# GpSimd makes the layer-norm scalings and the third bf16 parts of queries, keys and maxima, instead of VectorE

## The chip, the cores and the metric

One core of one Trainium2 chip runs the whole program. The metric is the device time of one execution in microseconds (us); the time of a kernel is the median of its runs.

## The reference

The reference is one transformer layer over 16 sequences of 512 tokens of 128 channels, in float32.

```
x = x + attention(layernorm(x))      # 16 heads of 8 channels, band |i - j| <= 128
x = x + ffn(layernorm(x))            # product-key experts: 8 heads, 32 x 32 keys, top 8 of 1024

attention:  softmax(q k^T / sqrt(8), masked to the band) v, then a 128x128 projection
layernorm:  (x - mean) / sqrt(var + 1e-5) over the 128 channels, no gain and no offset
ffn:        batch norm over all tokens, scores of 1024 experts in 8 heads, the best 8 of each,
            softmax weights times gelu of the expert products, summed
```

## The kernel before

The program has two stages that follow each other: `attention` (some 795 us of the profiled span), then `ffn`. The change touches `attention` alone.

`attention` is a software pipeline over sequences. Each engine has its own program, written out by hand; they meet through semaphores. Each engine runs steps t = -1 to 17 (t = 2 to 13 in a loop), and within a step 16 slots h = 0 to 15, one for each head. In step t three sequences are in work:

- sequence t: its scores (`scores`, L474 and L478) go to PSUM tiles SX and SY, and VectorE takes the row maxima of each head from them (two reductions, L395 and L397, in each slot). Each of the two PSUM tiles is single, so TensorE may write head h+1 into it only when VectorE has reduced head h.
- sequence t-1: its transposed scores (`scoresT`, L505) go to TX and TY, ScalarE takes the exponentials into PT (L340, L342), GpSimd sets what lies outside the band to zero (`mask`, L250, four instructions a head), and TensorE multiplies by the values (`values`, L531) for groups of four heads in slots 6, 10, 14 and 2 of the next step.
- sequence t+1 is prepared: layer-norm statistics (`stats`, slots 0 and 1), the variance to the power -1/2 on GpSimd (L258, slot 1), the scaling to xn (`norm`, L374, four instructions of 128x128, slot 3), the transposes of xn (slot 4), then the products q (slot 5) and k (slot 6). Sequence t-2 is finished: its attention output is divided by the softmax sums (L433, L435, slots 3, 7, 8 and 10), turned, projected, added to the input (L443), normalised again (`stats` in slot 13, L272 on GpSimd, `norm` in slot 14) and turned once more (slot 15).

Queries, keys and row maxima are used as sums of three bf16 parts, so that a bf16 product has the precision wanted. Part 1 is a rounding by ScalarE (L299, L351); VectorE subtracts it, which gives the rest (L421, L380); ScalarE rounds the rest to part 2 (L302, L353); VectorE subtracts once more and writes part 3 (L426 for q and k in slots 6 and 7, L383 for the maxima in slots 1 and 9). SyncE then stores the parts to memory and loads them back, rearranged, into Q and K (`back`, 24 transfers a step) and into three rows of Q (`shift_rows`). Each store waits for the third part.

All small products of a step (turned maxima, att0 to att3, xnT, q, k, at, pj, v, x2T) share one PSUM bank, MB. Each may write it only when the one before it in a fixed order has been read; that order is the list SHARED, and `bank_free` makes the wait. Here att0 (slot 3), read by L435, is ahead of xnT (slot 4); att1 (slot 7), read by L435, is ahead of att2 (slot 8).

Every engine works strictly in the order of its own program, so that a wait holds back all that is queued behind it.

Of the kernel before, what the change touches and what calls it, by code (L numbers as in the profile page):

```python
# [30 lines left out]
ALU = mybir.AluOpType  # L31
# [3 lines left out]
SEQS = 16  # L35
# [15 lines left out]
def attention(nc, ctx, x, w_qkvT, w_projT, identb, band, w_q, keysT, idf, bnst, KM, extra, x1_out, x2T_out):  # L51
# [186 lines left out]
    @block.gpsimd  # L238
    def _(pool):
        nc.gpsimd.memset(half[:, :], -0.5).then_inc(S["v_pads_set"], 1)  # L240
        for b in range(2):
            nc.gpsimd.memset(V[b][:, :, :, :], 0.0).then_inc(S["v_pads_set"], 1)
        pool.wait_ge(S["v_pads_set"], 3)
        for b in range(2):
            nc.gpsimd.memset(V[b][:, :, :, DK:DK + 1], 1.0).then_inc(S["v_pads_set"], 1)

        def mask(out, pairs, stop_low):

            s = 1 if stop_low else -1
            return nc.gpsimd.affine_select(out=out, in_=out, compare_op=ALU.is_ge, fill=0.0, base=0,  # L250
                                           pattern=([[0, 2]] if pairs else []) + [[s, P]], channel_multiplier=-s)

        def step(t, c):
            for h in range(H):

                if h == 1 and 0 <= c + 1 < SEQS:
                    pool.wait_ge(S["x_variance"], t + 2)
                    nc.gpsimd.tensor_tensor(rs[:, :], ve[:, :], half[:, :], ALU.pow).then_inc(S["x_rstd"], 1)  # L258

                if 0 <= c - 1 < SEQS:  # L260
                    pt = PT[:, h % 8, :]
                    y = pt[:, 512:1280].rearrange("p (j n) -> p j n", j=2)
                    await_(pool, S["outer_exp"], (t - 1) * H + h + 1)
                    mask(pt[:, 128:256], False, False).then_inc(S["exp_masked"], 1)
                    mask(pt[:, 256:384], False, True).then_inc(S["exp_masked"], 1)
                    await_(pool, S["inner_exp"], (t - 1) * H + h + 1)
                    mask(y[:, :, 0:128], True, True).then_inc(S["exp_masked"], 1)
                    mask(y[:, :, 256:384], True, False).then_inc(S["exp_masked"], 1)

                if h == 13 and 0 <= c - 2 < SEQS:  # L270
                    pool.wait_ge(S["x1_variance"], t - 1)
                    nc.gpsimd.tensor_tensor(trs[:, :], te[:, :], half[:, :], ALU.pow).then_inc(S["x1_rstd"], 1)  # L272

        steps(pool, step)

# [82 lines left out]
    def _(dve):  # L358
# [10 lines left out]
            dve.wait_ge(s2, (s + 1) * TILES)  # L369
            nc.vector.tensor_scalar(ae[:, :], av[:, :, 1], EPS, None, ALU.add).then_inc(to, 1)  # L370

        def norm(src, av, r, dst, to):
            for i in range(TILES):
                o = nc.vector.tensor_scalar(dst[:, i, :], src[:, i, :], av[:, i, 0:1], r[:, i:i + 1], ALU.subtract, ALU.mult)  # L374
            o.then_inc(to, 1)

        def shift(s, nth):

            dve.wait_ge(S["max_part1"], s * 2 + nth)
            nc.vector.scalar_tensor_tensor(out=rm[:, :].rearrange("p (i n) -> p i n", n=P), in0=MB[0:8, :, :], scalar=-1.0,  # L380
                                           in1=mp[:, 0, :].rearrange("p (i n) -> p i n", n=P), op0=ALU.mult, op1=ALU.subtract).then_inc(S["max_rest"], 1)
            dve.wait_ge(S["max_part2"], s * 2 + nth)
            nc.vector.tensor_tensor(mp[:, 2, :], rm[:, :], mp[:, 1, :], ALU.subtract).then_inc(S["max_part3"], 1)  # L383

        def step(t, c):
            b = c % 2
            for h in range(H):
                if 0 <= c < SEQS:
                    n = t * H + h + 1
                    dve.wait_ge(S["outer_scores"], n)  # L390
                    if h == 0 and c >= 1:
                        dve.wait_ge(S["maxima_turned"], t * 2 - 1)
                    if h == 8 and c >= 1:
                        dve.wait_ge(S["maxima_turned"], t * 2)
                    nc.vector.tensor_reduce(mx[:, h, 0:4:3], SX[:, :, :], AX.X, ALU.max).then_inc(S["outer_maxima"], 1)  # L395
                    dve.wait_ge(S["inner_scores"], n)
                    nc.vector.tensor_reduce(mx[:, h, 1:3], SY[:, :, 0:384], AX.X, ALU.max).then_inc(S["inner_maxima"], 1)  # L397

                if h == 1 and 0 <= c - 1 < SEQS:
                    shift(t - 1, 2)  # L400
                if h == 9 and 0 <= c < SEQS:
                    shift(t, 1)

                if h == 0 and 0 <= c + 1 < SEQS:
                    dve.wait_ge(S["x_loaded"], 16 * (t + 2))
                    stats(0, t + 1, xin[1 - b], st6, mv, ve, S["x_stats"], S["x_means"], S["x_variance"])
                if h == 1 and 0 <= c + 1 < SEQS:
                    stats(1, t + 1, xin[1 - b], st6, mv, ve, S["x_stats"], S["x_means"], S["x_variance"])
                if h == 3 and 0 <= c + 1 < SEQS:
                    dve.wait_ge(S["x_rstd"], t + 2)  # L410
                    if c >= 0:
                        dve.wait_ge(S["xn_turned"], t + 1)
                    norm(xin[1 - b], mv, rs, xn, S["xn_ready"])
                if c == -1 and h in (4, 7):

                    both = K[0 if h == 4 else 1][64:P, :, :].rearrange("p h n -> p (h n)").bitcast(F32)
                    nc.vector.memset(both, TWO_ONES).then_inc(S["k_ones_set"], 1)
                for hh, nm, dst, r, sc in ((5, "q", qp, rq, DK ** -0.5), (6, "k", kp, rk, 1.0)):
                    if h == hh and 0 <= c + 1 < SEQS:
                        dve.wait_ge(S[nm + "_part1"], t + 2)  # L420
                        nc.vector.scalar_tensor_tensor(out=r[:, :].rearrange("p (i n) -> p i n", n=P), in0=MB[:, :, :], scalar=sc,  # L421
                                                       in1=dst[:, 0, :].rearrange("p (i n) -> p i n", n=P),
                                                       op0=ALU.mult, op1=ALU.subtract).then_inc(S[nm + "_rest"], 1)
                    if h == hh + 1 and 0 <= c + 1 < SEQS:
                        dve.wait_ge(S[nm + "_part2"], t + 2)
                        nc.vector.tensor_tensor(dst[:, 2, :], r[:, :], dst[:, 1, :], ALU.subtract).then_inc(S[nm + "_part3"], 1)  # L426

                for i, sl in enumerate(ASLOT):
                    if h == sl and 0 <= c - 2 < SEQS:
                        n = (t - 2) * 4 + i + 1  # L430
                        dve.wait_ge(S["att_turned"], n)
                        hv = MB[:, :, :].rearrange("p g (h e) -> p (g h) e", e=SLOT_V)
                        nc.vector.reciprocal(rec[:, i, :], hv[:, :, DK]).then_inc(S["sums_inverted"], 1)  # L433
                        dve.wait_ge(S["sums_inverted"], n)
                        nc.vector.tensor_tensor(A[:, i, :].rearrange("p (h d) -> p h d", d=DK), hv[:, :, 0:DK],  # L435
                                                rec[:, i, :].unsqueeze(2).broadcast_to([P, H, DK]), ALU.mult).then_inc(S["att_normed"], 1)

                if h == 12 and 0 <= c - 2 < SEQS:
                    dve.wait_ge(S["projected"], t - 1)
                    dve.wait_ge(S["residual_loaded"], 16 * (t - 1))  # L440
                    if c - 2 >= 1:
                        dve.wait_ge(S["x1_stored"], 16 * (t - 2))
                    nc.vector.tensor_tensor(X1[:, :, :], MB[:, :, :], xres[:, :, :], ALU.add).then_inc(S["x1_ready"], 1)  # L443
                if h == 13 and 0 <= c - 2 < SEQS:
                    dve.wait_ge(S["x1_ready"], t - 1)
                    stats(0, t - 2, X1, t6, tv, te, S["x1_stats"], S["x1_means"], S["x1_variance"])
                    stats(1, t - 2, X1, t6, tv, te, S["x1_stats"], S["x1_means"], S["x1_variance"])
                if h == 14 and 0 <= c - 2 < SEQS:
                    dve.wait_ge(S["x1_rstd"], t - 1)
                    norm(X1, tv, trs, X2, S["x2_ready"])  # L450

            if 0 <= c - 2 < SEQS:
                dve.wait_ge(S["x2T_ready"], t - 1)
                nc.vector.bn_stats(bnst[:, t - 2, :] if isinstance(t, int) else bnst[:, bass.ds(t - 2, 1), :].rearrange("p o n -> p (o n)"), X2T[:, :]).then_inc(S["bn_stats_ready"], 1)
# [603 lines left out]
```

## Time and profile before

| | |
|---|---|
| median of 3 runs | 1863.76 us (1862.04 to 1866.11) |
| the profiled execution, its own time | 1866.48 us |
| its span | 1864.7 us |
| TensorE (PE) busy | 1573.5 us, 84% |
| VectorE (DVE) busy | 1521.5 us, 82% |
| ScalarE (ACT) busy | 1303.6 us, 70% |
| GpSimd (POOL) busy | 1329.2 us, 71% |

The shares are means over both stages. The page's slices show that from the third to the fifteenth slice of 40 (the full steps of `attention`) PE is busy for nine tenths or more, DVE for eight tenths, ACT for six and POOL for five; in `ffn` POOL is the fullest with nine tenths. A matmul's end is modelled in the profile and reaches past the start of the next one, so short stops of PE are read from the distance between starts, set against the same distance where nothing was awaited.

### The profile page before, as it was taken

Reading aid. Unit: us, or ns where it says so; the run is one execution under the profiler, and the core shown is the slowest. Engines: PE = TensorE matmul, PEld = TensorE weight load, DVE = VectorE, ACT = ScalarE, POOL = GpSimd, SP = SyncE. Lnnn points to the kernel's source line nnn. Section 1 sums busy time; section 2 is a strip of 40 time slices with the busy share of each in tenths; the row PEclk is TensorE's granted clock in tenths of the full one; section 3 lists DMA queues with packets and bytes.
Section 4 is the critical chain, followed back from the end, with each engine's and each line's share of the span. In section 5 each row is a group of like instructions: output and inputs, shape, how many; then the busy total and the mean of one; then the engine's idle time right before and its main releaser. Section 6 shows DMA issues by size and latency. Waiting matters only on the chain.

```text
span 1864.7 us, 38400 instructions
## 1 busy us (share of the span) xinstructions
PE 1573.5 (84%) x11936; PEld 1135.9 (61%) x11936; DVE 1521.5 (82%) x3784; ACT 1303.6 (70%) x1773; POOL 1329.2 (71%) x1579
## 2 busy tenths in 40 slices
PE   3899999999999999677887878788788787887877
PEld 2456566666666665346666666666666566666666
DVE  3778888888888886268898889888788898888888
ACT  1266666666666666368788787788778788787885
POOL 1055555555555555379999989989898898898995
PEclk9699999999999999789899999899899998998999
DMA  5334344444444442010000000000000000000000
GB/s 137 78 82 94 93 101 98 96 106 98 99 96 97 94 99 47 24 34 1 18 18 18 2 17 17 2 17 17 7 12 17 18 1 17 18 0 17 12 7 6
DMA packets 70876, 85.39 MB, mean 46 GB/s; under 512 B 6528, under 2 KB 61056, under 8 KB 66048
## 3 DMA queue, kind: packets, MB, share of 16 engines
q1 hardware_dynamic: 70752, 84.08, 19.2%
q8 instruction: 36, 0.59, 0.1%
q14 instruction: 88, 0.72, 0.1%
HBM read 58.10 MB, written 25.95 MB: 45 GB/s over the span
## 4 chain that ended last, share of the span: by engine, by line
DVE 18%; issue 17%; ACT 12%; PE 6%; POOL 3%; DVEq 1%; ACTq 0%; DMA 0%; POOLq 0%
DVE W L930 12%; ACT E L838 8%; PE WT L997 4%; POOL SUM L738 3%; ACT L773 2%; PE MB L940 2%; DVE M8Y L874 1%; DVE SMALL L891 1%; DVE SMALL L874 1%; DVE CT L913 1%; PE MB L943 1%; ACT L772 1%; ACT LZ L806 0%; PE E L953 0%; DVEq L698 0%
## 5 line engine op out<-in xcount | busy, mean ns | idle before, releaser
L738 POOL TENSOR_TENSOR SUM<-SIM 128x1024 f32<-128x1024 f32 x512 | 959.2, 1915 | 87.4 <-ACT SIM L766 77.7
L930 DVE SCALAR_TENSOR_TENSOR W<-SUM,SMALL,E 128x1024 f32<-128x1024 f32 x512 | 646.6, 1279 | 60.4 <-ACT E L838 51.7
L838 ACT ACTIVATE E<-SUM,NB 128x1024 f32<-128x1024 f32 x512 | 567.2, 1117 | 160.8 <-DVE W L930 120.2
L997 PEld LDWEIGHTS WT<-idf,W 128*128 128x128 f32 x4096 | 494.7, 150 | 232.6 <-issue 153.7
L997 PE MATMUL WT<-idf,W 128*128 128x128 f32 x4096 | 557.7, 289 | 78.7 <-DVE CT L913 57.0
L250 POOL TENSOR_SCALAR_AFFINE_SELECT PT<-PT 128x128 f32<-128x128 f32 (+1 forms) x1024 | 334.0, 352 | 314.0 <-ACT PT L340 280.0
L397 DVE TENSOR_REDUCE mx<-SY 128x2 f32<-128x768 f32 x256 | 242.5, 947 | 8.6 <-PE SY L478 8.4
L395 DVE TENSOR_REDUCE mx<-SX 128x2 f32<-128x512 f32 x256 | 175.2, 684 | 75.1 <-PE SX L478 74.4
L342 ACT ACTIVATE PT<-TY 128x768 f32<-128x768 f32 x256 | 207.6, 811 | 2.4 <-PE TY L505 0.7
L940 PE MATMUL MB<-KM,BNT 128*128 128x512 f32 x128 | 84.7, 748 | 121.1 <-ACT OUT L786 121.1
L340 ACT ACTIVATE PT<-TX 128x512 f32<-128x512 f32 x256 | 153.5, 600 | 45.0 <-PE TX L505 44.4
L474 PE MATMUL SY<-K,Q 72*128 72x384 bf16 x512 | 163.5, 342 | 10.8 <-DVE mx L397 10.5
L531 PE MATMUL PV<-PT,V 128*32 128x384 f32 (+1 forms) x2048 | 154.9, 444 | 2.3 <-POOL PT L250 2.3
L478 PE MATMUL SY<-bandb,idb 128*128 128x128 bf16 x1024 | 146.4, 225 | 0.0
L505 PE MATMUL TY<-Q,K 75*128 75x384 bf16 x512 | 127.1, 330 | 6.0 <-ACT PT L342 5.5
L943 PE MATMUL MB<-X2T,KI 128*128 128x512 f32 x240 | 128.0, 616 | 2.1 <-ACT SIM L766 1.9
L478 PEld LDWEIGHTS SY<-bandb,idb 128*128 128x128 bf16 x1024 | 103.8, 101 | 39.9 <-issue 6.1
L964 PE MATMUL MB<-KO,CT 128*128 128x128 f32 x1024 | 126.9, 278 | 1.1 <-DVE CT L913 1.1
L964 PEld LDWEIGHTS MB<-KO,CT 128*128 128x128 f32 x1024 | 121.7, 195 | 1.3 <-DVE CT L913 1.3
L474 PE MATMUL SX<-K,Q 72*128 72x256 bf16 x512 | 102.6, 282 | 18.3 <-DMA Q<-q_parts 14.9
L531 PEld LDWEIGHTS PV<-PT,V 128*32 128x32 f32 x2048 | 60.8, 111 | 83.1 <-issue 55.2
L319 ACT COPY U<-PV 128x512 f32<-128x512 f32 x64 | 37.4, 585 | 96.4 <-PE PV L531 96.4
(106 smaller groups left out, 1817.1 us busy)
## 6 DMA issues: line engine op xcount, KB each, us to landing
K<-k_parts SPq DMA_DIRECT2D x96, 192.0 KB
Q<-q_parts SPq DMA_DIRECT2D x288, 64.0 KB
q_parts<-qp SPq DMA_DIRECT2D x16, 384.0 KB, 2.4
k_parts<-kp SPq DMA_DIRECT2D x16, 384.0 KB, 2.4
xin<-in_x SPq DMA_DIRECT2D x16, 256.0 KB, 3.1
xres<-in_x SPq DMA_DIRECT2D x16, 256.0 KB, 9.3
x<-X SPq DMA_DIRECT2D x16, 256.0 KB, 2.2
x2T<-X2T SPq DMA_DIRECT2D x16, 256.0 KB, 2.1
```

The lines of the kernel that those rows point to most:

```text
L250: return nc.gpsimd.affine_select(out=out, in_=out, compare_op=ALU.is_ge, fill=0.0, base=0, pattern=([[0, 2]] if pairs else []) + [[s, P]], ...
L342: nc.scalar.activation(pt[:, 512:1280].rearrange("p (j n) -> p j n", j=2), TY[:, :, 0:384], ACT.Exp).then_inc(S["inner_exp"], 1)
L395: nc.vector.tensor_reduce(mx[:, h, 0:4:3], SX[:, :, :], AX.X, ALU.max).then_inc(S["outer_maxima"], 1)
L397: nc.vector.tensor_reduce(mx[:, h, 1:3], SY[:, :, 0:384], AX.X, ALU.max).then_inc(S["inner_maxima"], 1)
L474: pe.matmul(out, Q[b][0:KQ, h, i * P:(i + 1) * P], K[b][0:KQ, h, k0 * P:k1 * P], start=clear, stop=False, skip_group_check=True)
L478: return pe.matmul(out, idb[:, :], band_, start=False, stop=True, skip_group_check=True)
L531: o = pe.matmul(PV[32 * e:32 * e + 32, q0 * P:q1 * P], V[b][:, j, h, :], PT[:, h % 8, at:at + (q1 - q0) * P], start=(j == 0), stop=(j == 3 ...
L738: return eng.tensor_tensor(SUM[(q * FH + h) % RING][:, :].rearrange("p (i j) -> p i j", i=NK), sx, sy, ALU.add)
L838: nc.scalar.activation(E[h % 2][:, :], SUM[(k * FH + h) % RING][:, :], ACT.Exp, bias=NB[q][:, h:h + 1]).then_inc(S["exp_ready"], 1)
L930: nc.vector.scalar_tensor_tensor(out=W[h % WRING][:, :], in0=SUM[(k * FH + h) % RING][:, :], scalar=TOP[q][:, h, TOPK - 1:TOPK], in1=E[h % ...
L964: o = pe.matmul(po, CT[k % 2][:, e, :], key_out[:, e, :], start=False, stop=(e == BLK - 1))
L997: o = pe.matmul(WT[:, e, :], W[h % WRING][:, e * P:(e + 1) * P], ident[:, :], is_transpose=True, start=(h == 0 and e % 4 == 0), stop=(h == ...
```

## The change

The third parts (two for the maxima and one each for q and k in a step) and both layer-norm scalings (four instructions of 128x128 each) move from VectorE to GpSimd. No arithmetic changes. On GpSimd the scaling to xn stands in slot 2, the third part of the upper maxima behind it, both ahead of the masks of that slot; the third parts of q, k and the lower maxima stand ahead of the masks of slots 6, 7 and 10; the second power and the scaling to X2 stand ahead of the masks of slot 14 (the power stood behind those of slot 13, which is the same place). VectorE gets waits so that it does not overwrite what GpSimd still reads.

```diff
@@ gpsimd
+        def norm(src, av, r, dst, to):
+            for i in range(TILES):
+                o = nc.gpsimd.tensor_scalar(dst[:, i, :], src[:, i, :], av[:, i, 0:1], r[:, i:i + 1], ALU.subtract, ALU.mult)
+            o.then_inc(to, 1)
+
+        def shift(s, nth):
+
+            pool.wait_ge(S["max_part2"], s * 2 + nth)
+            nc.gpsimd.tensor_tensor(mp[:, 2, :], rm[:, :], mp[:, 1, :], ALU.subtract).then_inc(S["max_part3"], 1)
...
+                if h == 2 and 0 <= c + 1 < SEQS:
+                    if c >= 0:
+                        await_(pool, S["xn_turned"], t + 1)
+                    await_(pool, S["x_rstd"], t + 2)
+                    norm(xin[1 - (c % 2)], mv, rs, xn, S["xn_ready"])
+
+                if h == 2 and 0 <= c - 1 < SEQS:
+                    shift(t - 1, 2)
+                if h == 10 and 0 <= c < SEQS:
+                    shift(t, 1)
+                for hh, nm, dst, r in ((6, "q", qp, rq), (7, "k", kp, rk)):
+                    if h == hh and 0 <= c + 1 < SEQS:
+                        pool.wait_ge(S[nm + "_part2"], t + 2)
+                        nc.gpsimd.tensor_tensor(dst[:, 2, :], r[:, :], dst[:, 1, :], ALU.subtract).then_inc(S[nm + "_part3"], 1)
+
+                if h == 14 and 0 <= c - 2 < SEQS:
+                    pool.wait_ge(S["x1_variance"], t - 1)
+                    nc.gpsimd.tensor_tensor(trs[:, :], te[:, :], half[:, :], ALU.pow).then_inc(S["x1_rstd"], 1)
+                    if c - 2 >= 1:
+                        await_(pool, S["x2_turned"], t - 2)
+                    await_(pool, S["x1_rstd"], t - 1)
+                    norm(X1, tv, trs, X2, S["x2_ready"])
...
-                if h == 13 and 0 <= c - 2 < SEQS:
-                    pool.wait_ge(S["x1_variance"], t - 1)
-                    nc.gpsimd.tensor_tensor(trs[:, :], te[:, :], half[:, :], ALU.pow).then_inc(S["x1_rstd"], 1)
@@ vector
         def shift(s, nth):
 
             dve.wait_ge(S["max_part1"], s * 2 + nth)
+            prev = s * 2 + nth - 1
+            if not isinstance(prev, int) or prev >= 1:
+                dve.wait_ge(S["max_part3"], prev)
...
-            dve.wait_ge(S["max_part2"], s * 2 + nth)
-            nc.vector.tensor_tensor(mp[:, 2, :], rm[:, :], mp[:, 1, :], ALU.subtract).then_inc(S["max_part3"], 1)
...
                 if h == 1 and 0 <= c + 1 < SEQS:
+                    if c >= 0:
+                        dve.wait_ge(S["xn_ready"], t + 1)
                     stats(1, t + 1, xin[1 - b], st6, mv, ve, S["x_stats"], S["x_means"], S["x_variance"])
-                if h == 3 and 0 <= c + 1 < SEQS:
-                    dve.wait_ge(S["x_rstd"], t + 2)
-                    if c >= 0:
-                        dve.wait_ge(S["xn_turned"], t + 1)
-                    norm(xin[1 - b], mv, rs, xn, S["xn_ready"])
...
+                        if c >= 0:
+                            dve.wait_ge(S[nm + "_part3"], t + 1)
...
-                    if h == hh + 1 and 0 <= c + 1 < SEQS:
-                        dve.wait_ge(S[nm + "_part2"], t + 2)
-                        nc.vector.tensor_tensor(dst[:, 2, :], r[:, :], dst[:, 1, :], ALU.subtract).then_inc(S[nm + "_part3"], 1)
...
+                        dve.wait_ge(S["x2_ready"], t - 2)
...
-                if h == 14 and 0 <= c - 2 < SEQS:
-                    dve.wait_ge(S["x1_rstd"], t - 1)
-                    norm(X1, tv, trs, X2, S["x2_ready"])
```

## Rows read from the trace of the kernel before

**Rows 1.** Stretches by window: length, then busy us of each engine (instructions), PEclk.
```profile
391.29:435.23 43.94, 41.86 (x392) 27.04 (x392) 37.35 (x77) 28.86 (x49) 22.84 (x67) 1.00 0.43 98
```
**Rows 2.** Line L454, once a step: duration ns min/median/max, first and last start.
```profile
L454 DVEq FUSED_REGOPS  x12: 64/64/64, 169.5 to 652.7; - x12
```
**Rows 3.** Timeline of PE in that step: start us, us, engine, line, out<-in.
```profile
399.99 0.28 PE L478 MATMUL SY<-bandb,idb 128*128 128x128 bf16 x2
401.12 0.65 PE L558 MATMUL MB<-idf,xn 128*128 128x128 f32 x4 [0.85 <-DVE A L435]
...
402.96 0.28 PE L478 MATMUL SY<-bandb,idb 128*128 128x128 bf16 x2
403.07 1.08 PE L563 MATMUL MB<-xnT,wq 128*128 128x512 f32 x2
...
406.70 2.36 PE L531 MATMUL PV<-PT,V 128*32 128x256 f32 x32
...
412.20 0.28 PE L478 MATMUL SY<-bandb,idb 128*128 128x128 bf16 x2
412.93 0.66 PE L588 MATMUL MB<-idf,U 128*128 128x128 f32 x4 [0.45 <-DVE A L435]
...
431.82 0.61 PE L605 MATMUL MB<-idf,X 128*128 128x128 f32 x4
...
432.81 0.38 PE L474 MATMUL SX<-K,Q 72*128 72x256 bf16 x2
```
**Rows 4.** Timeline of DVE around the two stops of PE, and slot 14.
```profile
399.30 1.20 DVE L374 TENSOR_SCALAR xn<-xin,mv,rs 128x128 f32<-128x128 f32 x4
...
400.42 0.25 DVE L433 RECIPROCAL rec<-MB 128x16 f32<-128x16 f32 x1
400.69 0.29 DVE L435 TENSOR_TENSOR A<-MB,rec 128x128 f32<-128x128 f32 x1
...
411.55 0.83 DVE L426 TENSOR_TENSOR kp<-rk,kp 128x512 bf16<-128x512 f32 x1
...
412.58 0.29 DVE L435 TENSOR_TENSOR A<-MB,rec 128x128 f32<-128x128 f32 x1
...
430.49 1.12 DVE L374 TENSOR_SCALAR X<-X,tv,trs 128x128 f32<-128x128 f32 x4 [0.67 <-POOL trs L272]
```
**Rows 5.** Timeline in slots 1 and 2 (DVE, POOL) and slot 14 (POOL).
```profile
394.94 0.68 DVE L383 TENSOR_TENSOR mp<-rm,mp 8x512 bf16<-8x512 f32 x1 [0.69 <-ACT mp L353]
...
396.19 1.01 POOL L258 TENSOR_TENSOR rs<-ve,half 128x4 f32<-128x4 f32 x1 [3.55 <-DVE ve L370]
...
429.45 1.01 POOL L272 TENSOR_TENSOR trs<-te,half 128x4 f32<-128x4 f32 x1
```
**Rows 6.** Groups by line and form, whole span: busy us, mean ns.
```profile
L738 POOL TENSOR_TENSOR SUM<-SIM 128x1024 f32<-128x1024 f32 x512 | 959.2, 1915 | 87.4 <-ACT SIM L766 77.7 <-DVE W L930 9.6
...
L250 POOL TENSOR_SCALAR_AFFINE_SELECT PT<-PT 128x256 f32<-128x256 f32 x512 | 195.8, 406 | 33.6 <-ACT PT L342 28.0
L250 POOL TENSOR_SCALAR_AFFINE_SELECT PT<-PT 128x128 f32<-128x128 f32 x512 | 141.4, 297 | 280.3 <-ACT PT L340 280.0 <-issue 0.3
...
L426 DVE TENSOR_TENSOR kp<-rk,kp 128x512 bf16<-128x512 f32 x16 | 13.0, 815 | 0.0
...
L426 DVE TENSOR_TENSOR qp<-rq,qp 128x512 bf16<-128x512 f32 x16 | 10.9, 681 | 0.7 <-ACT qp L302 0.7
```
**Rows 7.** Timeline of the start: ACT, DVE, SyncE's queue (SPq) and PE.
```profile
17.80 0.62 ACT L302 CAST kp<-rk 128x512 bf16<-128x512 f32 x1 [0.76 <-DVE rk L421]
...
18.68 3.47 DVE L417 MEMSET K<- 64x4096 f32 x1 [0.91 <-issue]
22.18 0.69 DVE L426 TENSOR_TENSOR kp<-rk,kp 128x512 bf16<-128x512 f32 x1
...
39.80 0.59 PE L474 MATMUL SX<-K,Q 72*128 72x256 bf16 x2 [14.87 <-DMA Q<-q_parts]
```

More of the change, by code:

```diff
@@ L370, in stats @@
             nc.vector.tensor_scalar(ae[:, :], av[:, :, 1], EPS, None, ALU.add).then_inc(to, 1)
[L372 to L375, printed above, removed]
         def shift(s, nth):
             dve.wait_ge(S["max_part1"], s * 2 + nth)
+            prev = s * 2 + nth - 1
+            if not isinstance(prev, int) or prev >= 1:
+                dve.wait_ge(S["max_part3"], prev)
             nc.vector.scalar_tensor_tensor(out=rm[:, :].rearrange("p (i n) -> p i n", n=P), in0=MB[0:8, :, :], scalar=-1.0,
                                            in1=mp[:, 0, :].rearrange("p (i n) -> p i n", n=P), op0=ALU.mult, op1=ALU.subtract).then_inc(S["max_rest"], 1)
-            dve.wait_ge(S["max_part2"], s * 2 + nth)
-            nc.vector.tensor_tensor(mp[:, 2, :], rm[:, :], mp[:, 1, :], ALU.subtract).then_inc(S["max_part3"], 1)
         def step(t, c):
```

## The prediction

> **What bounds the kernel now.** I read the page's slices first: they split the run into `attention` and `ffn`, and the change leaves `ffn` as it is, so all that counts is the length of the attention steps. Next I took one full step by window [rows 1]: 43.94 us, with PE busy 41.86, DVE 37.35, ACT 28.86 and POOL 22.84. The start of the once-a-step line L454 says that this step is typical: 12 starts from 169.5 to 652.7 us are 11 distances of 43.93 us [rows 2]. PE is nearly full at a granted clock of 1.00, so a gain can only be what PE loses in stops. Then I went down PE's timeline of the step and compared distances between starts. Where nothing is awaited, the line of the last two mask products of a head (L478) is followed 0.11 us later by the next one (402.96 to 403.07 [rows 3]). From 399.99 to the transposes of xn it takes 1.13, so 1.02 us are lost; from 412.20 to the transposes of att2 it takes 0.73, so 0.62 are lost [rows 3]. Both lines name the division L435 on DVE as the releaser. Seven smaller excesses of the same kind, which I read off in the same way, are 0.05 to 0.4 us each; all together some 3.6 us a step, of which I count below only what the change reaches. That is the reading: PE sets the pace, and DVE stops it in two places.
>
> **What is taken from DVE.** Each step loses two scalings (1.20 and 1.12 us), the third parts of q and k (0.68 and 0.83) and two of the maxima (0.68 each) [rows 4 to 6], some 5 us, and with them the stops of DVE ahead of the maxima's part (0.69 [rows 5], twice) and ahead of the scaling in slot 14 (0.67 [rows 4]). Most of it buys nothing, as DVE waits for PE elsewhere. Where it counts:
> - Slots 3 and 4. The scaling to xn runs from 399.30 and pushes the reciprocal to 400.42 and L435 to 400.69 + 0.29 = 400.98; PE starts at 401.12, 0.14 later [rows 3, 4]. Without the scaling the pair of 0.56 us starts at about 399.3 and PE is released at 400.0, ahead of the 400.10 at which it would come. All 1.02 us go, if xn itself is there.
> - Slots 7 and 8. Without kp (from 411.55) L435 ends at 412.1 and not at 412.87 [rows 4], ahead of PE's 412.31. The 0.62 go.
> - Small stops behind L383 (0.09 in slot 3) and around slots 9 and 10 (0.06 to 0.14, four of them) go too, 0.45 together. But with DVE relieved, the next thing late is the chain ACT part 1, DVE rest, att3 around slots 9 and 10; I give 0.35 back for it, and 0.1 for others. Sum of this edit: 1.02 + 0.62 + 0.45 - 0.45 = 1.64 us a step.
>
> **What is put on POOL, and what waits for it.** No row shows a scaling on POOL. Nearest are its masks, one input and no scalar from memory: 297 ns for 128x128 and 406 for 128x256 [rows 6], and in a row of eight they follow each other faster than that. The other end is the power of 128x4, 1.01 us although it has four elements a row [rows 5], a fixed cost that a costly function can have. So a scaling is 0.26 to 1.0 us; I take c = 0.35, near the mask, whose shape it has, with something for two scalars. A subtraction of 512 elements is between the mask's rate (about 0.6 us) and the 1915 ns of a 128x1024 sum scaled by size with its fixed cost, 1.1 us [rows 6]; I take 1.05.
> - xn, slot 2. With L383 gone from DVE (394.94 to 395.6), the variance and thus the power come 1.3 us earlier, 394.9 in place of 396.19 [rows 5]. Then POOL masks head 1 until about 397.05, scales until 397.05 + 4c = 398.45, and PE can take it 0.15 later, against its 400.10. Free as long as c is below 0.72. Behind it wait the third part of the maxima (to 399.6) and the masks of heads 2 and 3, done by 402.3, where the value product takes them at 406.70 [rows 3]: 4 us of cover, so they cost nothing. If that cover were gone, each us late would be a us of PE.
> - X2, slot 14. This has no cover. The power ends at 429.45 + 1.01 = 430.46 [rows 5]; DVE then scaled until 431.61, PE turned X2 at 431.82 without waiting [rows 3, 4]. POOL is done at 430.5 + 4c, and PE released 0.15 later (by c = 0.35: 432.05). The stop is 4c - 1.17 us, here 0.23. The copy to X2T, and DVE's statistics on it ahead of its next reduction, move by the same amount, so it isn't counted twice.
> - Third parts of q and k. POOL comes to k's part behind the masks of head 6, some 0.6 us later than DVE did, q's 0.4. SyncE's stores, and the loads `back` behind them, go as much later. In the timeline of SyncE those loads are issued by 420 and the transfers thin out by 428.5, while PE's next step starts at 432.81 [rows 3]: 4 us of cover. The part of the lower maxima gets 2 us later; its store stands in the queue behind those same loads anyway. The part of the upper ones gets 4 us later, with a cover of 10 us until slot 8. All nothing.
> - The new waits on DVE (the previous third part, the previous scaling) are for things done a third of a step earlier, and cost nothing; behind them would stand the reductions.
>
> The SBUF page of the Trainium skill (SBUF — State Buffer, Who interferes with whom) says that a VectorE instruction with two SBUF inputs and a GpSimd instruction that reads SBUF block each other for the whole instruction. The trace agrees in kind: kp, which overlaps a mask, takes 815 ns, qp 681 [rows 6]. The change takes the last such instructions off DVE in these steps, so by the rule no new contention arises; it changes nothing in the sum.
>
> **The steps summed.** A full step: 1.64 - 0.23 = 1.4 us. Thirteen steps (t = 2 to 14) have both stops: 18.2 us. Steps 0 and 1 have the scaling without the division ahead of it: 1.5 together. In the start, kp's third part stands on DVE behind a memset from 18.68 (3.47 us) and runs at 22.18, though ACT had part 2 at 18.42 [rows 7]; the store of it, then the loads, then PE's first scores at 39.80 hang on it [rows 7]. On POOL, 0.3 us later for the scaling and 1.05 long, it is done at 19.9 and not 22.87: 2.5 us won, taking the loads to move with it. The last three steps lose the stop in slot 14 and its like in serial work: 1.0. Sum: 18.2 + 1.5 + 2.5 - 1.0 = 21.2 us. The profiled execution took 1866.48 us and would take 1845.3; it is 2.7 us above the median of the runs, 1863.76, and from that I get 1842.5 us, 1.1% less.
>
> **The rivals.**
> - GpSimd becomes the bound in slot 14, slower than before. The price is c: the stop 4c - 1.17 eats the 1.64 at c = 0.70, from there the kernel is slower. With c = 1.0, the row of the power, the stop in slot 14 is 2.8, and xn comes at 401.2, a stop of 1.1 where 1.02 was, so that of the 1.64 only 0.6 stays: 2.8 + 0.1 - 0.6 = 2.3 us a step, 30 in all, and some 8 in the last three steps: 1900. For it speaks only the power's row; against it the masks, which are whole instructions on 128x128 at 0.3. The GPSIMD Engine Reference of the Trainium skill (Engine selection) says to leave elementwise work to VectorE, GpSimd being about twice as slow with two inputs and near line rate with one; our two-input subtraction is covered, so by that page too slot 14 decides. Chance 0.13.
> - A middle c of 0.5 to 0.65: a stop of 0.8 to 1.4, 0.2 to 0.8 us won a step: 3 to 11 us and 1 to 2 from the start: 1852 to 1860. Chance 0.15.
> - The transfers become the bound: the cover of 4 us ahead of slot 0 is thinner than it looks, and PE waits for heads 0 to 7 what it had won. The window's DMA share of 0.43 [rows 1] is against it. Within 3 us of 1864. Chance 0.07.
> - The change doesn't do what it says, as GpSimd needs other code for scalings than for masks and loads it each time: two loads a step, no row has their price. In the trace POOL alternates between masks and powers with nothing between them, so I give it 0.03; slower by an unknown amount, over 20 us.
> - PE wins more: the stops of slots 1 and 2 behind DVE's reductions (0.41 and 0.34, from the timeline) go too. Up to 0.75 us in 13 steps: 1833. Chance 0.12.
> - The forecast, 1837 to 1850: 0.50.
>
> **Numbers.** A difference of 0.2% (3.7 us) is about what a measurement of this kernel can tell from none. Faster by more than that: 0.50 + 0.12 + nearly all of the middle case, 0.13: 0.75. Within it: 0.02 + 0.06: 0.08. Slower: 0.13 + 0.03 + 0.01: 0.17. The range has to leave out the slow rivals (0.16) and takes in the other cases: 1830 to 1862.
>
> **What would show it.** In the profile after: PE's transposes of xn and of att2 follow L478 after 0.11 us, with no stop named A; the step by L454 is 42.5 us; DVE busy in a step falls to about 32.5 and POOL rises to about 30; kp's third part is stored at about 20 us and the first scores start at 37. A scaling on POOL above 0.70 us, or a stop of PE ahead of the turned X2 of over 1.6 us, would show the forecast wrong; so would value products that wait for masks, or scores that wait for DMA.

## The result and the profile after

The changed kernel takes 1884.24 us in the median of its four runs, where the kernel before took 1862.9. One of the four, of 1918.5 us, ran in a slower state with a lower granted clock (0.913 against 0.937 to 0.942) and is left out of the ratio, so that 1881.47 us stands against 1862.9: 1.0096, with a 95% interval of 1.0069 to 1.0124. The change is slower by about 1%; the forecast was 1842.5, and the range ended at 1862. The profiled execution took 1881.47 us, its span is 1879.8.

The stages moved in opposite ways. The attention stage ends where the first instruction of `ffn` on VectorE starts: 795.5 us before, 816.5 after, 21.0 us later. `ffn`, whose code is the same, took 1069.2 us before and 1063.3 after. That second number moves by itself from kernel to kernel (more below), so what follows is about the 21 us.

The once-a-step line, which answers to [rows 2] (it is L472 now); columns: duration ns min/median/max, first and last start us:

```profile
L472 DVEq FUSED_REGOPS  x12: 64/64/64, 164.2 to 660.7; - x12
```

Eleven steps take 496.5 us, 45.14 each, where they took 43.93. The first start is 5.3 us earlier than before, so the start of the kernel gained the 4 us of the forecast and more, and the steps lost it. The groups by line and form, whole span (busy us, mean ns, idle before and its releaser), for what GpSimd got; they answer to [rows 6]:

```profile
L250 POOL TENSOR_SCALAR_AFFINE_SELECT PT<-PT 128x128 f32<-128x128 f32 x512 | 139.2, 293 | 154.7 <-ACT PT L368 154.5
...
L255 POOL TENSOR_SCALAR xn<-xin,mv,rs 128x128 f32<-128x128 f32 x64 | 50.3, 801 | 0.4 <-POOL rs L268 0.4
L255 POOL TENSOR_SCALAR X<-X,tv,trs 128x128 f32<-128x128 f32 x64 | 50.2, 798 | 3.4 <-POOL trs L286 3.4
...
L261 POOL TENSOR_TENSOR mp<-rm,mp 8x512 bf16<-8x512 f32 x32 | 36.8, 1149 | 5.6 <-ACT mp L381 5.6
...
L282 POOL TENSOR_TENSOR kp<-rk,kp 128x512 bf16<-128x512 f32 x16 | 18.6, 1162 | 3.7 <-ACT kp L330 3.7
...
L623 PE MATMUL MB<-idf,X 128*128 128x128 f32 x64 | 11.5, 310 | 38.1 <-POOL X L255 38.1
```

A scaling of 128x128 takes 0.8 us on GpSimd, nearly three masks of the same shape. The last row is the price: PE stood still for 38.1 us ahead of the transposes of X2 and waited for that scaling. One such place, in the timeline of PE and POOL (start us, us, engine, line, out<-in, idle before and its releaser), answers to slot 15 in [rows 3] and to slot 14 in [rows 4, 5]:

```profile
388.03 1.03 POOL L286 TENSOR_TENSOR trs<-te,half 128x4 f32<-128x4 f32 x1
389.27 3.14 POOL L255 TENSOR_SCALAR X<-X,tv,trs 128x128 f32<-128x128 f32 x4 [0.21 <-POOL trs L286]
...
390.29 0.28 PE L496 MATMUL SY<-bandb,idb 128*128 128x128 bf16 x2
...
392.56 0.63 PE L623 MATMUL MB<-idf,X 128*128 128x128 f32 x4 [1.99 <-POOL X L255]
```

Slots 3 and 4, and att2, in the same views, answer to the two stops in [rows 3]:

```profile
401.76 3.14 POOL L255 TENSOR_SCALAR xn<-xin,mv,rs 128x128 f32<-128x128 f32 x4
...
404.55 0.28 PE L496 MATMUL SY<-bandb,idb 128*128 128x128 bf16 x2
404.96 0.66 PE L576 MATMUL MB<-idf,xn 128*128 128x128 f32 x4
...
416.01 0.28 PE L496 MATMUL SY<-bandb,idb 128*128 128x128 bf16 x2
416.13 0.60 PE L606 MATMUL MB<-idf,U 128*128 128x128 f32 x4
```

The distance ahead of att2 is 0.12 us, the free one; ahead of xn it is 0.41 where it was 1.13. Both stops that VectorE made are gone as forecast; at xn a stop of 0.3 us is left, which GpSimd makes. From one turned X2 to the next (392.56 to 437.04) it is 44.48 us; but the mean step is 45.14. The difference is in the granted clock. Rows by window: length, busy us (instructions) of PE, PEld, DVE, ACT and POOL, then PEclk (1.00, 0.50, 1.00), DMA share, GB/s:

```profile
200.00:209.00 9.00, 7.47 (x78) 4.88 (x75) 6.48 (x16) 4.88 (x8) 6.65 (x14) 1.00 0.32 80
211.00:220.00 9.00, 9.00 (x53) 5.32 (x54) 7.22 (x17) 4.66 (x8) 4.81 (x13) 0.50 0.71 143
222.00:231.00 9.00, 8.94 (x72) 5.94 (x72) 7.02 (x11) 7.26 (x13) 7.30 (x19) 1.00 0.15 27
```

From 210.7 to 221 us TensorE ran at 0.50, 1.2 GHz in place of 2.4. The stop before it ended at 209.46. The step from there to the next turned X2 (257.33) took 47.87 us, 3.4 more than the 44.48 of a step without a fall; the steps with the falls at 163.0 and 258.5 us took 46.77 and 46.26, 2.3 and 1.8 more. In the kernel before there is no such fall from 100 to 740 us; in the changed one there are four, at 163.0, 210.7, 258.5 and 705.7, each 0.3 to 2 us behind a stop of 1.99 us (162.69, 209.46, 257.33, 703.84), and one more behind that of 749.95. The nine stops between were followed by none. These counts, like those of every kernel below, are from one profiled execution.

### The profile page after: what moved, and what is told of

Same layout as the page of the kernel before. It is cut to its first block, busy times and chain, and to the rows that moved or that the text cites. A ratio compares the mean times of both kernels' runs of the same rounds, so it can differ in the third digit from the quotient of the medians.

```text
span 1879.8 us, 38549 instructions
## 1 busy us (share of the span) xinstructions
PE 1575.7 (84%) x11936; PEld 1139.1 (61%) x11936; DVE 1447.0 (77%) x3592; ACT 1304.9 (69%) x1773; POOL 1494.7 (80%) x1771
## 4 chain that ended last, share of the span: by engine, by line
issue 14%; DVE 14%; POOL 12%; ACT 9%; PE 6%; DVEq 0%; ACTq 0%; POOLq 0%; DMA 0%
POOL SUM L756 12%; DVE W L948 9%; ACT E L856 6%; PE WT L1015 3%; PE MB L958 2%; ACT L791 2%; DVE M8Y L892 1%; DVE SMALL L909 1%; PE MB L961 1%; DVE SMALL L892 1%; DVE CT L931 1%; PE E L971 0%; ACT LZ L824 0%; ACT SIM L784 0%; ACT L790 0%
## 5 line engine op out<-in xcount | busy, mean ns | idle before, releaser
L1015 PEld LDWEIGHTS WT<-idf,W 128*128 128x128 f32 x4096 | 486.5, 148 | 226.5 <-issue 149.4
L1015 PE MATMUL WT<-idf,W 128*128 128x128 f32 x4096 | 550.4, 286 | 72.2 <-DVE CT L931 52.8
L250 POOL TENSOR_SCALAR_AFFINE_SELECT PT<-PT 128x128 f32<-128x128 f32 (+1 forms) x1024 | 328.1, 350 | 178.2 <-ACT PT L368 154.5
L523 PE MATMUL TY<-Q,K 75*128 75x384 bf16 x512 | 131.0, 339 | 5.6 <-ACT PT L370 5.3
```

What stands on the lines that cost most here:

```text
L1015: o = pe.matmul(WT[:, e, :], W[h % WRING][:, e * P:(e + 1) * P], ident[:, :], is_transpose=True, start=(h == 0 and e % 4 == 0), stop=(h == ...
```

## The experiments

Theory A: the whole loss is the scaling to X2. Nothing covers it in slot 14, it stops TensorE for 2 us, and a stop like that can be followed by a fall of the clock. Rival B: it is GpSimd's load as a whole, with the later third parts and stores. Rival C: the clock falls for a reason of its own.

**e1 and e9: X2 back on VectorE.**

```diff
@@ gpsimd, slot 14
...
-                    await_(pool, S["x1_rstd"], t - 1)
-                    norm(X1, tv, trs, X2, S["x2_ready"])
@@ vector
...
+                if h == 14 and 0 <= c - 2 < SEQS:
+                    dve.wait_ge(S["x1_rstd"], t - 1)
+                    norm(X1, tv, trs, X2, S["x2_ready"])
```

> The changed kernel, but the scaling to X2 is made by VectorE in slot 14 again; the scaling to xn and the third parts stay on GpSimd. Theory A (the whole loss is the scaling to X2: a scaling on GpSimd takes 0.78 us and not 0.35, nothing covers it in slot 14, TensorE stops 1.99 us there, and after such a stop its clock sometimes falls to half): no stop over 0.3 us ahead of the turned X2, no stretch at half clock in the full steps, a step of about 42.5 us in place of 44.5, and the prediction's sum without its slot-14 term: about 1840 us. Rival B (it is GpSimd's load as a whole, or the later third parts and their stores): most of the loss stays, 1865 to 1880 us.

Measured: 1854.96 us, ratio 0.9926 (0.9901 to 0.9952). The step is (628.4 - 163.4) / 11 = 42.27 us, from the once-a-step line:

```profile
L475 DVEq FUSED_REGOPS  x12: 64/64/64, 163.4 to 628.4; - x12
```

There is no stop of 1 us or more in the full steps and no fall between 100 and 720 us; att2 and X2 are released without a stop, and xn costs PEld 0.3:

```profile
DVE X L398 <- POOL trs L286: 5.5, 8, 0.7
...
PEld MB L579 <- POOL xn L255: 2.1, 8, 0.3
```

These are waits from 280 to 620 us (total, times, longest); the first is VectorE's 0.7 us for the power, as before. All of the mechanism came as theory A says, and B falls: one scaling moved back turns a loss of 1% into a gain. But the total is 15 us above the expected 1840 (10 by the ratio, as the kernel before took 1867.59 us beside it): the attention stage ended 24.3 us earlier (771.2), and `ffn` took 1078.4 us in place of 1069.2. In this run and the next ones a ratio is to the kernel before as it ran beside them.

**e2: X2 alone on GpSimd**, the rest as in the kernel before.

> The kernel before with the scaling to X2 alone moved to GpSimd. Theory A: the two stops that VectorE made (1.02 and 0.62 us) stay, and 1.95 us are added: a step of 45.9 us, 25 us in 13 steps, some 6 in the last ones, and 3.3 for each fall of the clock (2 to 5 of them): 1898 to 1912 us. Rival B: with GpSimd's load but a third of that added by the change and the stores where they were, close to 1863 us, at most 1870.

Measured: 1944.92 us, ratio 1.0432 (1.039 to 1.0473). The direction is A's, the size is not. A step without a fall is 46.13 us (219.02 to 265.15), 2.2 above before, as expected. But ten of the twelve stops from 169 to 711 us have a fall in their last 0.3 us or up to 1.2 us behind, not 2 to 5 in all, and each costs 1.9 to 5.2 us (360.89 to 408.93 is 48.04; 169.37 to 219.02 is 49.65; 505.18 to 556.49 is 51.31). The mean step is 49.2. So falls are most of this kernel's loss, and how many there are does not follow from the length of the stop, which is the same 1.95 us here as in the changed kernel with 4 of 13. In the rows one sees a stop, and the matmuls behind it at 1.5 to 1.7 times their length, with twice the distance from start to start (0.42 from TX to TY, where a step without a fall has 0.22):

```profile
556.49 1.09 PE L618 MATMUL MB<-idf,X 128*128 128x128 f32 x4 [1.95 <-POOL X L255]
557.37 0.64 PE L518 MATMUL TX<-Q,K 75*128 75x256 bf16 x2
557.79 0.85 PE L518 MATMUL TY<-Q,K 75*128 75x384 bf16 x2
...
265.62 0.38 PE L518 MATMUL TX<-Q,K 75*128 75x256 bf16 x2
265.84 0.49 PE L518 MATMUL TY<-Q,K 75*128 75x384 bf16 x2
```

**e3: only the third parts on GpSimd.**

> The changed kernel with both scalings back on VectorE; only the third parts are made by GpSimd. Theory A: the stop of 0.62 us ahead of att2 goes and the 1.02 ahead of xn stays, a step of about 43.3 us, 8 us in 13 steps, and some 3 at the start, as k's third part no longer stands behind the memset: about 1852 us. Rival B (later third parts hold back the stores and loads): 1863 us or more, with TensorE waiting for DMA ahead of slot 0 or 8.

Measured: 1857.45 us, ratio 0.9948 (0.9926 to 0.997); the step is 43.05 us, 0.25 shorter than expected. Its profiled execution took 1843.41 us, the fastest of the six, so that the profile shows more gain than the median. In the full steps TensorE doesn't wait for DMA ahead of any slot. The later third parts cost nothing.

**e4 and e6: the stop filled with work.** e4 has 16 transposes of the identity ahead of the wait for X2, e6 four products of 128x512 (this is e6's edit):

```diff
                     bank_free(pe, "x2T", t, c)
+                    for i in range(4):
+                        pe.matmul(MB[:, :, :], idf[:, :], KT[:, :], start=True, stop=True)
                     pe.wait_ge(S["x2_ready"], t - 1)
```

> The changed kernel, with 16 transposes of the identity (some 1.8 us of TensorE work whose result is overwritten) in slot 15 between the wait for the bank and the wait for X2, so that TensorE works through the stop. Theory A with the stop as the cause of the clock's fall: no stretch at half clock in the full steps, the step stays at about 44.5 us, and the 3.3 us of each fall are won: 1866 to 1874 us. Rival C (the clock falls there for another reason): falls as before, 1880 to 1887 us.

> The changed kernel with its stop filled again, but by four products of 128x512 in place of 16 transposes, so that TensorE's program grows by 8 instructions a slot 15 and not by 32. In e4 the program's growth brought a stop of 2.6 us without a releaser at the loop's end, with a fall behind it, where the filled stops had none. Theory A: no such stop here, no falls in the full steps, a step of 44.5 us, and of the changed kernel's loss the part of the falls (4 or 5 of 3.4 us) is won: 1.000 to 1.004 of the kernel before. If the falls come whatever fills the stop: 1.01.

Measured: e4 1894.59 us, ratio 1.0137 (1.0111 to 1.0162); e6 1898.93 us, ratio 1.0189 (1.0143 to 1.0236). Neither won anything, and both lie above what either theory expected. In e6 the filling was mis-sized: a product of 128x512 in f32 is two passes (the "x2" of L563 in [rows 3] is one product), so it ran for 3.65 us and not for 1.84. And both bring a new stop that names no releaser, in each second step, behind slot 15 of the loop's last step. In e4:

```profile
208.36 1.92 PE L622 MATMUL MB<-idf 128*128 128x128 f32 x16
210.40 0.66 PE L625 MATMUL MB<-idf,X 128*128 128x128 f32 x4
210.90 0.38 PE L523 MATMUL TX<-Q,K 75*128 75x256 bf16 x2
211.12 0.49 PE L523 MATMUL TY<-Q,K 75*128 75x384 bf16 x2
214.28 0.61 PE L492 MATMUL SX<-K,Q 72*128 72x256 bf16 x2 [2.68 <-issue]
```

As a clean test of the filling they fail, yet they tell about the clock. In e4 there are five falls between 200 and 600 us, and five stops of the new kind (2.5 to 2.7 us): each fall is with one of them, and the filled places, in the steps between too, have none. GpSimd has no part in these stops. In e6 the new stops are 1.1 to 1.7 us, five of them, with three falls, behind the longer three (1.39, 1.39, 1.68).

**e5, e7, e8: the length of the scaling to X2 as a dial.** e5 shares it, two tiles on each engine at once. e7 makes it in two instructions of 128x512 with broadcast operands. e8 scales by constants (subtract 0, multiply by 1), so that it leaves the normalising of X2 out and its result is not the layer's. This is e7's edit:

```diff
-                    norm(X1, tv, trs, X2, S["x2_ready"])
+                    nc.gpsimd.tensor_tensor(X2[:, :, :], X1[:, :, :], tv[:, :, 0:1].broadcast_to([P, TILES, P]), ALU.subtract).then_inc(S["x2_centred"], 1)
+                    await_(pool, S["x2_centred"], t - 1)
+                    nc.gpsimd.tensor_tensor(X2[:, :, :], X2[:, :, :], trs[:, :].unsqueeze(2).broadcast_to([P, TILES, P]), ALU.mult).then_inc(S["x2_ready"], 1)
```

> The changed kernel, with the scaling to X2 shared: two tiles on GpSimd and two on VectorE, at the same time. Theory A (the stop is 4c - 1.17 us with c = 0.78, and falls of the clock follow stops of about 2 us): with 2c in place of 4c and the 0.17 that GpSimd waits for its own power, the stop is 0.5 to 0.6 us, the step 42.27 (e1) + 0.55 = 42.8 us, no falls in the full steps: some 8 us above e1, 0.995 to 0.999 of the kernel before. Were the loss from moving any of the scaling off VectorE, and not from its length, it would be near the changed kernel, 1.01.

> The changed kernel, with the scaling to X2 on GpSimd as two instructions of 128x512 (subtract the mean, then multiply, each with a broadcast operand) in place of four of 128x128. From the 1.15 us that a third part takes, and 0.2 for the wait between the two: 2.5 us in place of 3.14, a stop of about 1.35 us in place of 1.99, a step of 43.9 us. If a broadcast operand costs more, up to 3.5 us and a longer stop.

> The changed kernel, with the scaling to X2 by constants (subtract 0, multiply by 1) and not by two scalars from memory, so X2 is the unscaled sum. It asks what the 0.8 us of a scaling are. If reading the two scalars makes them, an instruction falls to the 0.3 us of a 128x128 mask, the scaling to X2 ends before TensorE wants it, no stop in slot 15, a step near 42.3 us. If it is the operation itself, 0.7 to 0.8 us and the stop of 1.99 stay. The four on xn keep their scalars, for comparison.

The three kernels, with the changed one and e1 around them; the stop is the idle time of PE ahead of X2's transposes:

| kernel | scaling to X2 on GpSimd | stop | step | falls, 150 to 710 us | ratio to before |
|---|---|---|---|---|---|
| after | 4 x 0.78 = 3.14 us | 1.99 | 44.48 without a fall, 45.14 mean | 4 | 1.0096 |
| e8 | 4 x 0.62 = 2.48 us | 1.31 | 43.80 | 0 | 1.001, a single run |
| e7 | 1.04 + 0.2 + 1.04 = 2.28 us | 1.06 | 43.53 | 0 | 1.0006, a single run |
| e5 | 1.71 us | 0.55 | 43.12 | 0 | 0.9957 (0.9936 to 0.9978) |
| e1 | none | 0 | 42.27 | 0 | 0.9926 (0.9901 to 0.9952) |

The dial is straight over the first four rows: the step less the stop is 42.49, 42.49, 42.47 and 42.57 us. e1, with no stop, lies 0.2 to 0.3 us below that line, which is not explained. A scaling of 0.78 us gives 44.48, above the 43.93 of before; one of 0.62 gives 43.80, below it. e7's halves are cheaper than expected (1.04, not 1.15) and its single run of 1862.25 us is the time of the kernel before, 1861.19 beside it; e8's is 1863.06. For e8 the answer to its question is: mostly the operation itself. Without scalars from memory an instruction is 643 ns and not 798; the mask's 0.3 us isn't reached:

```profile
L255 POOL TENSOR_SCALAR xn<-xin,mv,rs 128x128 f32<-128x128 f32 x64 | 50.1, 794 | 0.4 <-POOL rs L268 0.4
L291 POOL TENSOR_SCALAR X<-X 128x128 f32<-128x128 f32 x64 | 39.7, 643 | 3.2 <-POOL trs L286 3.2
```

**e10: the scaling to xn in two instructions**, X2 on VectorE; and e9, the kernel of e1 again beside it.

> The kernel of e1 once more, on another chip and in 5 rounds. In e1's profile the attention stage ended 24.4 us earlier than before, but the whole was only 15 us shorter, since the ffn stage, the same code, took 1078 us and not 1069. If that length is drawn anew in each execution (over the profiles so far it goes from 1062 to 1078 with its mean granted clock, 0.94 to 0.924), this profile shows the same attention stage, 771 us, and another ffn, 1062 to 1072, and the ratio comes out at about 0.988. If an earlier and fuller attention stage makes ffn slower, ffn is again near 1078 and the ratio 0.9926.

> e1 with the scaling to xn, on GpSimd, as two instructions of 128x512 with a broadcast operand, as e7 had for X2 (2.3 us in place of 3.13). TensorE's last stop there, 0.3 us ahead of the transposes of xn, goes; a step of 42.0 to 42.1 us in place of 42.27 and 0.8 us at the start: 3 to 4 us less than e9.

Measured: e9 1852.19 us, ratio 0.9922 (0.9894 to 0.995); e10 1846.27 us, ratio 0.9899 (0.9873 to 0.9926). e10's step is (620.8 - 158.8) / 11 = 42.0 us, as expected; PE waits no more for xn, and it is 6 us faster than e9 where 3 to 4 were expected. (In the two profiled executions the difference is 2 us: the attention stage is 8 shorter and `ffn` 6 longer.) In e9 the attention stage ended at 769.8 and `ffn` took 1075.5 us; in e10 761.6 and 1081.7. The long `ffn` of e1 is no accident of one execution: e9 is the same kernel.

**e11 and e12: a pause ahead of `ffn`**, e10 with memsets on VectorE between the stages.

> e10 with a pause of some 7 us (8 memsets on VectorE that nothing needs) between the attention stage and ffn. In the profiles of e1, e9 and e10, whose attention ended at 771, 770 and 762 us, ffn took 1078, 1076 and 1082 us, in all others, whose attention ended between 773 and 875, it took 1062 to 1071. If only the moment at which ffn starts decides (how its stops fall against the clock), the ffn behind the pause is shorter or longer by luck, at any rate not 1082 again. If the fuller attention stage makes ffn slower, ffn is 1078 to 1084 again, and the whole 7 us above e10: 1853 us.

> The same with a pause of some 21 us (24 memsets), in which TensorE has next to nothing to do. If a rest of TensorE ahead of ffn is what gives it a better clock, ffn is 1062 to 1070 us and half or more of the pause comes back: 1853 to 1860 us. If the moment of the start decides, ffn is as in the kernels whose attention ended at about 785: 1065 to 1070. If the fuller attention stage decides and a pause changes nothing, ffn stays near 1080 and the whole is 1867 us.

Measured: e11 1842.77 us, ratio 0.9879 (0.9848 to 0.991); e12 1859.92 us, ratio 0.9982 (0.9966 to 0.9999). The pauses came out at 9 and 28 us, as each memset and its wait took 1.17. The windows of `ffn` in e10 and in e11 (columns as above):

```profile
761.60:1843.30 1081.70, 867.62 (x5632) 690.54 (x5632) 915.17 (x2566) 837.94 (x1003) 959.84 (x514) 0.92 0.04 12
```

```profile
774.70:1840.65 1065.95, 855.52 (x5626) 678.92 (x5626) 915.00 (x2566) 835.51 (x999) 960.01 (x513) 0.93 0.04 12
```

With a useless pause of 9 us `ffn` took 1066 us and not 1082, and the kernel was no slower; with 28 us it took 1064, and about half of the pause was lost (by the ratios 15 us against e10, by the profiles 12). The engines other than PE are equally busy in both rows, and PE is less so at the higher clock. So it is not the fuller attention stage that makes `ffn` slow. Whether it is the rest, or merely the moment at which it starts, these two can't tell: both pauses change both. (The attention of e3 ended at 773.4 us, hardly later than e1's, and its `ffn` took 1068.1.)

## Why the prediction was wrong, step by step

**The reading of the bound held.** PE sets the pace, DVE stopped it in two places, and both stops went with the work. Without slot 14 the prediction gave 1.64 us a step; e1 measures 43.93 - 42.27 = 1.66, and e10, where the rest of the stop at xn is gone as well, 1.93. That e1 meets 1.64 so closely is partly luck: it still has the 0.3 us at xn, and won as much elsewhere beyond the sum. VectorE's busy time in a step fell to 32.51 us as forecast; GpSimd's rose to 33.04 where 30 was forecast, which is the price below. In the views by window, as above:

```profile
392.56:437.04 44.48, 41.62 (x393) 27.27 (x393) 32.51 (x64) 28.92 (x48) 33.04 (x79) 1.00 0.43 97
```

**The covers held.** Masks, stores and loads got later, and nobody waited: PEld's wait for the masks is 5.3 us from 280 to 620 us, before and after, and e3 shows no wait for DMA in the steps. The new waits of DVE show up nowhere.

**The step that failed is one term: the price c of a scaling on GpSimd.** The prediction took 0.35 us, near the mask, out of 0.26 to 1.0; it is 0.78. The form of the term was right. With the measured c the stop 4c - 1.17 is 1.95 us, and PE stood 1.99 idle. Both are past what the prediction named as signs against it, 0.70 and 1.6 us. The point from which the change loses was put at 0.70; e8 at 0.62 gains 0.13 us a step, the change at 0.78 loses 0.55. The rival with that mechanism had a chance of 0.13, by which the two bounds were not treated alike: the mask was nearest in shape, but a scaling is another operation, and its row existed nowhere. The third parts were sized well (1.05 forecast, 1.15 measured), since a row of the same operation was there.

**The falls of the clock were not in the sum at all.** With c right it would have given 0.3 + 1.95 - 1.64 = 0.6 us a step and some 6 in the last three steps, less 4 for the start and steps 0 and 1: about 1873 us. The changed kernel is 8 above that, at 1881.47. Of the 21.0 us that its attention stage lost in the profile, the falls are more than half. The first turned X2 came 5.5 us earlier than before (162.69 against 168.2). The twelve steps behind it took 541.2 us and not 527.0: 6.6 more by the longer step, 7.5 by three falls. From there to the end it was 112.7 us and not 100.3. In e8, whose stop is 0.68 us shorter, that end took 105.4; with three longer stops this makes 107.5, so that by this estimate some 5 us are left for the last two falls and 7 for the stops, near the 6 above. The falls are then 12 to 13 us together, and `ffn` was 6 us shorter. The prediction let a stop cost its own length. What is shown: from 150 to 710 us, in the one profiled execution of each kernel, falls stand only close to stops (up to 2.1 us behind their end) of 1.39 us or more, made by GpSimd (after, e2) or by nobody named (e4, e6), and there is none in the kernels whose stops are at most 1.31 (before, e1, e3, e5, e7, e8, e9, e10). Outside of these steps, where TensorE is less full, every kernel has falls, e10's from 711.0 us on, and some with no stop of 1 us near (720.8 us in e1, 123.7 in e8), so that rival C is against the rows for the full steps alone. That e2's many falls are no accident of its profile is seen in its four runs: their mean granted clocks are 0.908 to 0.917, and those of the kernel before beside them 0.942 to 0.949. What is not: why 4 of 13 stops are followed by one in the changed kernel and 10 of 12 in e2. e2 also keeps the two stops of 1.02 and 0.62 us that VectorE makes; whether they matter here was not tried.

**The start gained about as forecast.** k's third part ended at 20.72 + 1.16 = 21.9 us and not at 19.9, since the scaling ahead of it was longer; PE's first scores came at 37.87, 1.9 us earlier where 2.5 were forecast, and by the first turned X2 it was 5.5.

**`ffn` was taken as constant.** It is the same code, and went from 1062.4 (e2) to 1081.7 us (e10). Part of the gain of e1, e9 and e10 was given back there, 6 to 12 us; a pause of 9 us gets it back, and why remains open.

The Trainium skill was cited for blocking between VectorE with two SBUF inputs and GpSimd (SBUF — State Buffer, Who interferes with whom). The step before had one such place, and the mask of 128x128 that ran beside kp there took 458 ns, where no other took over 293. After the change no such pair is left in the step, and the longest of these masks is 299 ns, so the trace agrees in direction. In size it shows less than a block for the whole instruction: the mask was some 0.17 us longer, and kp 0.13 longer than qp. The same page says that a VectorE instruction in a two-port mode also holds the shared pair; whether VectorE's scaling ran in such a mode, no trace shows. In e5 the two engines scale at the same time, and of GpSimd's two instructions the one beside VectorE takes 931 ns and the other 788 (timeline, then the view of the line, with its shortest, median and longest):

```profile
465.30 0.61 DVE L402 TENSOR_SCALAR X<-X,tv,trs 128x128 f32<-128x128 f32 x2 [0.69 <-POOL trs L286]
465.47 1.71 POOL L255 TENSOR_SCALAR X<-X,tv,trs 128x128 f32<-128x128 f32 x2 [0.21 <-POOL trs L286]
...
L255 POOL TENSOR_SCALAR X<-X,tv,trs x2: 788/860/931, 465.5 to 466.4; 128x128 f32<-128x128 f32 x2
```

The rule of the Trainium skill's GPSIMD Engine Reference (Engine selection), GpSimd near line rate with one input, is not borne out: four scalings take 3.13 us there and 1.12 on VectorE [rows 4].

## What to carry to other kernels

Before moving an operation to another engine, look for a row of that very operation there; if there is none, write the sum as a function of its price and ask at the place without cover where it turns, and give the far bound its due. Move what has slack at the place where it stands: the third parts were free and the scaling to xn nearly so (0.3 us a step), the scaling to X2, with 1.2 us between its input and its reader, was not, and taking back that one alone gives a kernel 0.7 to 0.8% faster than before, or 1.0% with xn in two instructions. And a stop of some 2 us on a full TensorE can cost two to nearly four times its length, as the clock may fall close behind it (1.99 and 1.8 to 3.4 us in the changed kernel, 1.95 and 1.9 to 5.2 in e2).

## What the runs showed of the hardware that was not expected

- On GpSimd a subtract and multiply of 128x128 takes 0.8 us with two scalars from memory and 0.64 with constants, against 0.29 for a mask of that shape. Two instructions of 128x512 with a broadcast operand (1.04 us each) do the same work as four scalings in 2.28 us in place of 3.13.
- Falls to half clock in a TensorE that is otherwise full: seen only close to stops of 1.39 us or more, 1.8 to 5.2 us each, in the worst kernel at ten of twelve stops.
- 16 (e6) or 32 (e4) more instructions, matmuls and weight loads together, in a slot 15 of TensorE's loop brought a stop of 1.1 to 2.7 us without a releaser once a turn of the loop. What it is was not tried.
- A pause of 9 us between two stages made the second 16 us shorter in the profile, and the whole kernel no slower. Why is open.
